# A windowed-attention block: the MLP's way down as unsplit 128x32 tiles, its residual in four VectorE operations

## The reference

```python
x = shortcut + out                       # out: attention over windows, projected
h1 = jax.nn.gelu(_ln(x, norm2_w, norm2_b) @ mlp_w1.T + mlp_b1, approximate=False)
x = x + (h1 @ mlp_w2.T + mlp_b2)
...
denom_sq = jnp.einsum('nchw,ic->nihw', x * x, gamma_eff) + beta_eff[None, :, None, None]
return x * jax.lax.rsqrt(denom_sq)
```

## Time and profile before

| | |
|---|---|
| runs of the kernel, us | 1768.22, 1769.26, 1774.46 (median 1769.26) |
| span of the profiled execution | 1766.9 us, 81406 instructions |
| PE, PEld busy | 1720.2 (97%), 1252.8 (71%) |
| VectorE busy | 1629.6 (92%) |
| ScalarE busy | 1527.5 (86%) |
| GpSimd busy | 1356.5 (77%) |
| mean granted TensorE clock | 0.993 |

### The profile page before, as it was taken

The page is one execution under the profiler, slowest core; times in us unless marked ns, Lnnn a source line. Parts: engine busy times, 40 slices in busy tenths (PEclk is TensorE's granted clock), DMA queues, the critical chain, the costliest instruction groups (busy, mean ns, idle before and its releaser), DMA issues.

```text
span 1766.9 us, 81406 instructions
## 1 busy us (share of the span) xinstructions
PE 1720.2 (97%) x32612; PEld 1252.8 (71%) x32612; DVE 1629.6 (92%) x4508; ACT 1527.5 (86%) x2832; POOL 1356.5 (77%) x1532
## 2 busy tenths in 40 slices
PE   4999999999999999999999999999999999999996
PEld 2677777777777777777777777777777777777763
DVE  5899999999999999999999999999999999999983
ACT  2798998988898988988898888998888898998986
POOL 3478878878878878878778877888878878878862
PEclk9999999999999999999999999999999999999997
DMA  2122122122122122122122122122122122122111
GB/s 58 27 46 52 37 54 52 37 54 53 37 53 52 36 54 52 38 53 52 36 55 52 36 55 50 37 56 52 35 56 49 37 56 51 37 55 52 28 32 27
DMA packets 215154, 81.35 MB, mean 46 GB/s; under 512 B 116118, under 2 KB 214780, under 8 KB 214780
## 3 DMA queue, kind: packets, MB, share of 16 engines
q1 hardware_dynamic: 214218, 76.04, 19.7%
q10 hardware_dynamic: 562, 0.11, 0.0%
HBM read 25.75 MB, written 25.17 MB: 29 GB/s over the span
## 4 chain that ended last, share of the span: by engine, by line
PE 96%; DVE 1%; issue 1%; ACT 1%; DMA 0%; SPq 0%; POOL 0%; POOLq 0%; DVEq 0%
PE mm_bank L999 49%; PE score_banks L1058 8%; PE score_banks L947 7%; PE mm_bank L1105 6%; PE mm_bank L1032 5%; PE pv_bank L1081 5%; PE turn_banks L939 5%; PE turn_banks L953 3%; PE mm_bank L1094 3%; PE mm_bank L1091 3%; PE score_banks L1066 1%; PE mm_bank L1134 0%; DMA x_ext<-in_x 0%; DVE stats L767 0%; SPq L378 0%
## 5 line engine op out<-in xcount | busy, mean ns | idle before, releaser
L457 POOL TENSOR_TENSOR hidden_lo<-hidden,hidden_hi 128x512 fp32r<-128x512 f32 x378 | 480.9, 1286 | 0.0
L618 ACT ACTIVATE hidden<-mm_bank 128x512 f32<-128x512 f32 x381 | 227.8, 598 | 124.1 <-PE mm_bank L999 111.8
L539 ACT ACT_TABLE_LOAD x253 | 324.6, 1283 | 4.5
L452 POOL TENSOR_SCALAR y_hi<-y 96x512 fp32r<-96x512 f32 x128 | 108.1, 845 | 206.8 <-ACT y L563 206.8
L812 DVE TENSOR_REDUCE row_max<-score_banks 128x8 f32<-128x512 f32 x384 | 250.8, 681 | 10.8 <-PE score_banks L1066 8.1
L820 DVE TENSOR_TENSOR shifted<-score_banks,row_max 128x512 f32<-128x512 f32 x384 | 250.7, 680 | 0.0
L469 POOL TENSOR_TENSOR x_sq<-x 96x512 f32<-96x512 f32 x126 | 130.8, 1038 | 152.2 <-DVE x L846 152.2
L585 ACT ACTIVATE probs<-shifted 128x512 f32<-128x512 f32 x384 | 236.2, 627 | 10.6 <-DVE shifted L820 3.4
L452 POOL TENSOR_SCALAR hidden_hi<-hidden 128x512 fp32r<-128x512 f32 x378 | 229.8, 619 | 1.3 <-ACT hidden L618 1.3
L597 ACT ACTIVATE probs_t<-score_banks 128x512 f32<-128x512 f32 x384 | 215.1, 602 | 0.0
L767 DVE BATCH_NORM_STATS2 stats<-turn_banks 128x6 f32<-128x96 f32 x1024 | 191.1, 248 | 17.1 <-PE turn_banks L939 17.1
(11 more groups left out here) (132 smaller groups left out, 4489.2 us busy)
## 6 DMA issues: line engine op xcount, KB each, us to landing
x_ext<-in_x SPq DMA_DIRECT2D x128, 192.0 KB, 2.9
k_block<-k SPq DMA_DIRECT2D x768, 32.0 KB
out<-o_ext SPq DMA_DIRECT2D x128, 192.0 KB, 2.6
w_raw<-in_w_t SPq DMA_DIRECT2D x1, 144.0 KB
w<-in_w_t SPq DMA_DIRECT2D x1, 144.0 KB
qkv_raw<-in_qkv_t ACTq DMA_DIRECT2D x1, 108.0 KB
ident_sb<-in_ident SPq DMA_DIRECT2D x1, 64.0 KB, 2.2
q_quadrants<-in_qmask SPq DMA_DIRECT2D x3, 1.0 KB
```

The source lines that it names most:

```text
L452: nc.gpsimd.tensor_scalar(hi, whole, 1.0, 1.0, ALU.mult, ALU.mult).then_inc(hi_ready, 1)
L457: nc.gpsimd.tensor_tensor(lo, whole, hi, ALU.subtract).then_inc(is_split, 1)
L539: nc.scalar.preload_act_table_set(name)
L618: nc.scalar.activation(hidden_of(A)[:, n, :], up_bank(A, n), ACT.Gelu).then_inc(gelu_ready, 1)
```

## The change

The way down is no longer split. GpSimd's `split_hidden` goes, and with it the tiles hidden_hi, hidden_lo, w2_hi and w2_lo and their semaphores. PE multiplies `hidden` by `w2` in float32, as 128x32 tiles: for each chunk three matmuls of 384 columns, one for each group of 32 output rows, on PSUM partitions 0 to 95; the last 128 tokens go to partitions 96 to 127, in a quarter of the bank for each group of rows, and are summed over the chunks there. The way down waits once for the three gelus of its half, and gelu for the way down of the half before. The second residual reads the bank in four operations. The last two halves stay as they were.

```diff
-MLP_WEIGHTS = 3
+MLP_WEIGHTS = 2
...
-                run(split_hidden, SETTLE)
...
             def gelu(A, a, n):
                 if n == 0 and A < FINAL:
-                    wait(act, hidden_split, HID_CHUNKS * A)
+                    wait(act, mlp2_made, A)
...
             def second_residual(A, a):
                 dve.wait_ge(mlp2_made, A + 1)
                 wait(dve, out_ready, A - 1)
+                to, x = half_of(x3, a), half_of(x2[:, unit_slot(a), :], a)
+                if A < FINAL - 1:
+                    for g in range(HEAD_PAIRS):
+                        rows = slice(32 * g, 32 * g + 32)
+                        nc.vector.scalar_tensor_tensor(to[rows, MAIN:HALF],
+                                                       mm_bank("mlp2", A)[DIM:128, g * 128:(g + 1) * 128],
+                                                       b2_col[rows, :], x[rows, MAIN:HALF], ALU.add, ALU.add)
+                    nc.vector.scalar_tensor_tensor(to[:, 0:MAIN], mm_bank("mlp2", A)[0:DIM, 0:MAIN],
+                                                   b2_col[:, :], x[:, 0:MAIN], ALU.add, ALU.add)\
+                        .then_inc(x3_ready, 1)
+                    return
...
             def mlp_down(A, a, n):
                 if n == 0:
                     mm_wait("mlp2", A)
-                pe.wait_ge(hidden_split, HID_CHUNKS * A + n + 1)
-                made = in_parts(mm_bank("mlp2", A)[0:DIM, :], w2_hi[:, n, :], w2_lo[:, n, :],
-                                hidden_hi[:, n, :], hidden_lo[:, n, :],
-                                first=(n == 0), last=(n == HID_CHUNKS - 1))
+                if n == 0:
+                    pe.wait_ge(gelu_ready, HID_CHUNKS * (A + 1))
+                for g in range(HEAD_PAIRS):
+                    rows = slice(32 * g, 32 * g + 32)
+                    nc.tensor.matmul(mm_bank("mlp2", A)[rows, 0:MAIN], w2[:, n, rows], hidden[:, n, 0:MAIN],
+                                     start=n == 0, stop=n == HID_CHUNKS - 1)
+                rows = slice(32 * n, 32 * n + 32)
+                for c in range(HID_CHUNKS):
+                    made = nc.tensor.matmul(mm_bank("mlp2", A)[DIM:128, n * 128:(n + 1) * 128], w2[:, c, rows],
+                                            hidden[:, c, MAIN:HALF], start=c == 0, stop=c == HID_CHUNKS - 1)
                 if n == HID_CHUNKS - 1:
                     made.then_inc(mlp2_made, 1)
```

More of the change, by code:

```diff
@@ L99, in window_block @@
         w1_hi, w1_lo = (sb(f"w1_{part}", [DIM + 1, HIDDEN], f32r) for part in ("hi", "lo"))
-        w2_hi, w2_lo = (sb(f"w2_{part}", [128, HID_CHUNKS, DIM], f32r) for part in ("hi", "lo"))
         wgdn = sb("wgdn", [DIM + 1, DIM])
@@ L135, in window_block @@
         hidden = sb("hidden", [128, HID_CHUNKS, HALF])
-        hidden_hi = sb("hidden_hi", [128, HID_CHUNKS, HALF], f32r)
-        hidden_lo = sb("hidden_lo", [128, HID_CHUNKS, HALF], f32r)
         x3 = sb("x3", [DIM, UNIT])
@@ L204, in window_block @@
         gelu_ready = sem("gelu_ready")
-        hidden_hi_ready = sem("hidden_hi_ready")
-        hidden_split = sem("hidden_split")
         mlp2_made = sem("mlp2_made")
@@ L476, in rest_of_squares @@
                 split_lo(x3_sq_hi[0:DIM, :], x3_sq_lo[0:DIM, :], x3_sq[0:DIM, :], sq_hi_ready, sq_split, A + 1)
[L478 to L491, removed]
             def wrap_out(A, a):
@@ L517, in _ @@
             rounds(steps)
-            late(split_hidden, FINAL - 2)
             late(wrap_out, FINAL - 4)
@@ L738, in _ @@
             mlp_in_parts = ((wgdn_hi[:, :], wgdn_lo[:, :], wgdn[:, :]),
-                            (w1_hi[:, :], w1_lo[:, :], w1[:, :]),
-                            (w2_hi[:, :, :], w2_lo[:, :, :], w2[:, :, :]))
+                            (w1_hi[:, :], w1_lo[:, :], w1[:, :]))
             assert len(mlp_in_parts) == MLP_WEIGHTS
```

## The result

The changed kernel takes 1880.46 us (median of four runs, 1879.69 to 1886.77) against 1769.2: slower, with a ratio of 1.063, 95% interval 1.061 to 1.065. The forecast was 1877, with a range of 1842 to 1905.

What follows compares the result with a forecast made beforehand. PE was taken to bound the round, VectorE 0.1 to 0.35 us behind. Afterwards the later of VectorE's list and the bank cycle decides: 126 x 0.86 = +108 us, giving 1877, range 1842 to 1905.

Steps and rivals of the forecast that it cites:

- the tie over the bank: PE's first way-up matmul waits for the second residual's bank, hand-back 0.14 us; a later residual moves PE by as much.
- PE, way down: Nine f32r matmuls of 2.17 us a half become f32 tiles of about 2.01: gain 0.06 to 0.16, taken as 0.10.
- VectorE, residual: Second residual in four operations: small ones 0.35 us each (0.31 to 0.36), the large one 0.61.
- The lost overlap in front: On VectorE, before the first small residual operation: overlap of 0.08 with L795 lost and 0.01 more, +0.09 us.
- The rule of the Trainium skill on held instructions: VectorE: an operation starting in another 32-partition group waits for all earlier ones; all four residual operations held, L838 not.
- The VectorE limit: VectorE's own list alone: 12.26 + 0.09 + 3 x 0.35 + 0.53 = 13.93 us a round, +0.90 for a short one.
- the coupled cycle: Hand-back 0.15, PE way up through way down 12.12 less 0.10, 0.23 to VectorE, residual 1.66: 14.06 us, +0.86.
- GpSimd and ScalarE: Removing 710.7 us of GpSimd's split work gains nothing, since PE never waits for it; gelu's changed waits also cost nothing.
- (a): Rival: PE still decides and the residual hides; 8 to 20 us shorter, about 1757. Chance 0.04.
- (b): Rival: the residual's small operations overlap on VectorE, stepping 0.20 us; +0.36 a round, +45, 1814. Chance 0.07.
- (c): Rival: way-down tiles on PE don't run side by side, 4.5 us instead of 2.17; +414, 2183. Chance 0.04.
- (d): Rival: PE, idling about 1 us a round, falls to 1.2 GHz for a quarter of its work; about 2170. Chance 0.03.

Runs made afterwards that it cites:

- e1: The kernel before, split way down kept, with only the second residual changed to three 32x128 and one 96x384 operation: 1892.26 us, ratio 1.069.
- e2: The changed kernel without the residual's three 32x128 operations, only the 96x384 one, last quarter of x3 left zero: 1773.41 us, ratio 1.002.
- e5: The changed kernel with the three small residual operations reading and writing partitions 0 to 31, so none changes partition group: 1835.95 us, ratio 1.036.
- e6: The changed kernel with the output's multiplication moved from VectorE to GpSimd, first in GpSimd's round: 1874.5 us, ratio 1.059.

## Why the prediction was right

*The bound before.* PE bounded the round, with VectorE 0.1 to 0.35 us behind, and the tie over the bank was tight: e1, VectorE's part alone, costs the residual's whole growth. Of the rounds taken for the sum, 13.03 isn't the usual short one; the row left out between them, 927.06 to 940.18, has 13.12, the median, and half of the rounds are long, not two thirds.

*PE, way down.* The term was -0.10 us a round. The way down itself is 0.07 shorter (1009.15 to 1011.25, 2.10), within the bounds of 0.06 to 0.16, and tiles that add up over chunks run side by side as the sums' do: two neighbouring starts of L1114 are 0.32 apart, as L1091's second pass. What I left out is the projection, which loses the same again, 0.94 instead of 0.87 (1011.25 to 1012.19). I had looked for the change of kind only at the way down's own edges. e2 shows the net where PE bounds: nothing, or 4 us of loss. It didn't hurt the forecast, since the projection runs beside the residual, and PE waits for the hand-back behind it anyway.

*VectorE, residual.* The small operation was taken at 0.35 with an upper bound of 0.36; it is 353 ns and steps by 0.37. The large one was 0.61 and is 613 ns. The lost overlap in front was 0.09 and is 0.11 (996.62 to 997.33 less 0.60). L815 follows the large one after 0.54, overlapping, as was assumed and no row could show. So the surplus of the scalar form is in the fixed part. The rule of the Trainium skill on held instructions (VectorE: DVE Perf Modes, section on two Vector instructions with no wait between them) gave the same picture, and e5 agrees with it: with no change of partition group the three starts are 0.26 apart.

*The bound afterwards.* The VectorE limit was 13.93 and the short round is 13.99; the coupled cycle was 14.06, e6 shows it at 14.06, and the long round is 14.08. Per round the forecast was +0.86 to +0.90, and measured are 0.87 for the short and 0.86 for the long ones. The mechanism is the forecast's, two limits that take turns, but that the numbers meet so closely is partly luck. In the cycle three terms were off and cancel: PE from the way up to the way down's end takes 12.06 (999.19 to 1011.25) and not 12.02, the residual 1.71 and not 1.66, and VectorE starts 0.14 behind the way down's end (e6) and not 0.23. In the VectorE limit the residual and the step in front of it are 0.08 longer (1.64 to L815's start against 1.58, 0.71 against 0.69) and the rest of the list 0.02 shorter. Against a short round of 13.12 the limit's +0.90 would have been +0.81. And VectorE's wait in a long round was expected at the residual, for the way down; it is at the row maxima, for the scores.

*The range.* Its lower end was added up wrongly: with a small operation of 0.31 and 0.16 saved the long round's 13.88 is +0.68, not +0.66, and 13.81 over 13.03 is +0.78, not +0.74, so the sum would be 1859 instead of 1857. The range was then widened to 1842, and nothing hangs on it.

*GpSimd and ScalarE.* Costed at nothing. e1 against the changed kernel leaves room for 12 us at most, in favour of the change, and the 0.10 us a round that the tiles were to save make up 12.6.

*The rivals.* (a) needed a residual within 0.35 us more; it is 0.97. (b) fell with the steps of 0.37, though e5's 0.26 shows that three fifths of the way from the forecast's step of 0.35 to (b)'s 0.20 is the partition group. (c) fell with L1114's three tiles starting together at 1009.15, L1118's behind them from 1009.17, and a way down of 2.10 us. (d) fell with a granted clock of 1.00 in both windows.

*What it said the profile would show.* PE's share near 92% is 93%, GpSimd 649 us, the wait in front of the way up is there with 0.66 a round. VectorE near 97% busy is 96% in the two rounds shown (13.49 of 13.99, 13.57 of 14.08) and 93% on the page, which takes in the start, the end and the few rounds that are longer; before, the same difference stood between 96% in a round (12.64 of 13.20) and the page's 92%.

## What to carry to other kernels

A matmul form is paid for where its result is read: the column tiles cost PE nothing here, and the quarter that lands on other partitions cost VectorE 1 us a half, where the tiles could save PE 0.16 at most by the prediction's own bounds. Where two banks are handed round, add the reader's time to every cycle over the hand-back and not only to the reader's own sum; here, taking 66 us of other work from the reader's engine bought back 6. And an engine with much idle time has it at one place: look where, before giving it work.

## What was not expected of the hardware

The projection, a full-width float32 matmul of two passes, takes 0.94 us behind 128x32 tiles and 0.87 behind full-width float32r matmuls. And a small operation of the residual whose input or output starts in another group of 32 partitions than the one ahead of it costs about 0.1 us more of VectorE's time than one that doesn't (0.37 against 0.26 a step, with 353 against 331 ns a piece), so of 1 us that the residual lost, 0.3 was in where the data lay.
